# Four more split pairs, and four normalisations moved from VectorE to ScalarE, in a fused embedding, attention and mixture-of-experts kernel

## The reference, cut to what matters

```python
h = concat(fine_table[ids], softmax(cluster_table.T[ids] + b) @ coarse_table)
a = layernorm(h)                                   # x1 in the kernel
xn = rms_norm(a)
x2 = a + mem_scale * decayed_linear_attention(xn)
xn2 = rms_norm(x2)
h = h + x2 + op_scale * gelu(xn2 @ read_mix + bias) @ write_w
x3 = layernorm(h)
gates = normalised top-6 of softmax(x3 @ router_w.T + router_b)   # 64 experts, each with a capacity
out = h + sum over experts and 2 shared ones of gate * down(silu(x3 @ w_gate) * (x3 @ w_up))
```

## Time and profile before

| | |
|---|---|
| median of 3 runs | 718.52 us (718.14 to 718.71) |
| span of the profiled execution, first to last instruction | 716.0 us |
| what lies around the span, median less span | 2.5 us |
| busy: PE, PEld, DVE, ACT, POOL | 692.8, 524.7, 523.4, 350.6, 466.5 us |
| mean granted TensorE clock | 0.995 of full speed |

### The profile page before, as it was taken

How to read it: one execution, slowest core, us unless ns; L and a number is a source line. 1 busy time by engine, 2 the same in 40 slices (tenths; PEclk the granted TensorE clock), 3 DMA queues, 4 the chain that set the end, 5 groups by cost and what they waited for, 6 DMA issues and landing times.

```text
span 716.0 us, 9975 instructions
## 1 busy us (share of the span) xinstructions
PE 692.8 (97%) x3133; PEld 524.7 (73%) x3133; DVE 523.4 (73%) x1074; ACT 350.6 (49%) x609; POOL 466.5 (65%) x345
## 2 busy tenths in 40 slices
PE   7788899999999999999999999999999999999998
PEld 7666677777777777777777777777777777777775
DVE  5677686987768867887769877788678766674444
ACT  3543455446454374445553474544745435534432
POOL 5035477776677767685676776676775656676664
PEclk9999999999999999999999999999999999999999
DMA  5504232243323333333333433333333433334431
GB/s 204 226 1 128 71 118 104 85 133 105 111 106 114 114 108 99 120 113 102 118 103 101 128 103 103 118 110 109 114 105 102 125 103 105 115 112 124 138 123 60
DMA packets 48869, 80.17 MB, mean 112 GB/s; under 512 B 9520, under 2 KB 13744, under 8 KB 48816
## 3 DMA queue, kind: packets, MB, share of 16 engines
q1 hardware_dynamic: 47792, 77.44, 33.4%
q0 software_dynamic: 1024, 2.10, 1.2%
HBM read 76.35 MB, written 3.15 MB: 111 GB/s over the span
## 4 chain that ended last, share of the span: by engine, by line
PE 88%; DVE 4%; issue 3%; POOL 2%; ACT 1%; DVEq 0%; POOLq 0%
PE bank_y L467 16%; PE bank_g L481 8%; PE bank_g L482 8%; PE bank_g L483 8%; PE bank_u L483 8%; PE bank_u L481 8%; PE bank_u L482 8%; PE bank_y L464 4%; PE bank_y L462 4%; PE bank_y L461 4%; POOL hid L1040 1%; PE bank_f L408 1%; PE bank_f L386 1%; PE bank_f L402 1%; PE bank_f L445 1%
## 5 line engine op out<-in xcount | busy, mean ns | idle before, releaser
L1040 POOL TENSOR_TENSOR hid<-hid,gate_rows 128x512 f32<-128x512 f32 x256 | 374.2, 1470 | 195.4 <-DVE hid L881 193.0
L623 ACT ACTIVATE hid<-bank_g 128x512 f32<-128x512 f32 x264 | 156.6, 599 | 264.4 <-PE bank_g L483 261.8
L881 DVE TENSOR_TENSOR hid<-hid,bank_u 128x512 f32<-128x512 f32 x264 | 178.7, 681 | 128.3 <-PE bank_u L483 78.2
L481 PE MATMUL bank_g<-x_hi,gate_hi 128*128 128x512 f32 x264 | 142.9, 541 | 0.0
L467 PE MATMUL bank_y<-hid,w_down 128*128 128x512 f32 x272 | 138.7, 591 | 0.0
L887 DVE TENSOR_TENSOR hid_lo<-hid,hid_hi 128x512 fp32r<-128x512 f32 x128 | 110.2, 861 | 2.4 <-ACT hid_hi L629 2.4
L482 PE MATMUL bank_g<-x_hi,gate_lo 128*128 128x512 f32 x264 | 104.5, 396 | 0.0
L483 PE MATMUL bank_g<-x_lo,gate_hi 128*128 128x512 f32 x264 | 104.5, 396 | 0.0
L481 PE MATMUL bank_u<-x_hi,up_hi 128*128 128x512 f32 x264 | 103.9, 393 | 0.1
L483 PE MATMUL bank_u<-x_lo,up_hi 128*128 128x512 f32 x264 | 103.8, 393 | 0.0
L482 PE MATMUL bank_u<-x_hi,up_lo 128*128 128x512 f32 x264 | 103.8, 393 | 0.0
(11 more groups left out here) (209 smaller groups left out, 857.1 us busy)
## 6 DMA issues: line engine op xcount, KB each, us to landing
gate_rows<-gates_dram SPq DMA_DIRECT2D x512, 128.0 KB, 2.9
w_down<-down_t_dram SPq DMA_DIRECT2D x3, 704.0 KB, 14.5
out_dram<-later SPq DMA_DIRECT2D x7, 256.0 KB, 3.1
hid<-gate_t_dram SPq DMA_DIRECT2D x2, 704.0 KB, 5.8
gates_dram<-gates_t SPq DMA_DIRECT2D x8, 128.0 KB, 2.2
gate_rows<-up_t_dram SPq DMA_DIRECT2D x1, 704.0 KB, 5.7
later<-up_t_dram SPq DMA_DIRECT2D x1, 704.0 KB, 9.9
raw<-gate_t_dram SPq DMA_DIRECT2D x1, 704.0 KB, 11.0
```

The lines of the kernel that those rows point to most:

```text
L481: pe.matmul(o, w_hi[name][:, p, :], x3_hi[par][:, :], start=True, stop=False)
L623: act.activation(hid[:, slot(par, p), :], bank_g[(p + par) % 2][:, :], ACT.Silu).then_inc(sem("silu"), 1)
L881: dve.tensor_tensor(hid[:, s, :], hid[:, s, :], bank_u[(p + par) % 2][:, :], ALU.mult)\
L1040: pool.tensor_tensor(hid[:, s, :], hid[:, s, :], gate_rows[:, row, :], ALU.mult)\
```

## The change

Pairs 8, 12, 18 and 20 become split pairs too, so 20 of 33 are; the slots of `hid_hi` and `hid_lo` go by the running number of the split pair, still with two slots. `down_hi` and `down_lo` are made in nine pieces instead of one. For all sequences but the first, `x1`, `xn2` and `x3`, and from the third sequence on `xn`, are made by ScalarE activations (scale and bias are columns), at iterations 3, 11, 19 and 0. An activation adds its bias after it scales, so VectorE also makes the negated means, and GpSimd multiplies them by `inv1` or `inv3` into `shift1` and `shift3`. One run of filler in the prologue (`WARM_PREP`) grows from 9 transposes to 22.

```diff
-SPLITS = PAIRS // 2
+SPLIT_PAIRS = tuple(sorted(tuple(range(1, PAIRS, 2)) + (8, 12, 18, 20)))
+SPLITS = len(SPLIT_PAIRS)
...
-ACT_AT = dict(xn_hi=2, y_hi=4, z=6, ...
+ACT_AT = dict(xn=0, x1=3, xn2=11, x3=19, xn_hi=2, y_hi=4, z=6, ...
...
-WARM_START, WARM_PREP, WARM_EXP, WARM_COARSE, WARM_GATES = 20, (2, 9), 4, 26, 20
+WARM_START, WARM_PREP, WARM_EXP, WARM_COARSE, WARM_GATES = 20, (2, 22), 4, 26, 20
...
+        def split_runs():            # yields (slots, pairs) of each evenly spaced run: nine of them
+            at = 0
+            for _, group in itertools.groupby(enumerate(SPLIT_PAIRS), lambda jp: jp[1] - 2 * jp[0]):
+                pairs = [p for _, p in group]
+                yield slice(at, at + len(pairs)), slice(pairs[0], pairs[-1] + 1, 2)
+                at += len(pairs)
         def is_split(p):
-            return p % 2 == 1
+            return p in SPLIT_PAIRS
+        def split_slot(b, p):
+            return (SPLITS * b + SPLIT_PAIRS.index(p)) % SPLIT_RING
+        def split_slot_freed(b, p):
+            n = SPLITS * b + SPLIT_PAIRS.index(p) - SPLIT_RING
+            return PAIRS * (n // SPLITS) + SPLIT_PAIRS[n % SPLITS] + 1 if n >= 0 else 0
...                                   # act_late
+            if p == ACT_AT["xn"] and b > 1:
+                act.wait_ge(sem("shift1"), b)
+                for t in range(TILES):
+                    last = act.activation(xn[:, t, :], emb[par][:, t, :], ACT.Identity,
+                                          bias=shift1[:, 1, t:t + 1], scale=inv1[:, 1, t:t + 1])
+                last.then_inc(sem("xn"), 1)
+            if p == ACT_AT["x1"] and b:
...                                   # waits for shift1 and the x2 before; x1 with inv1[:, 0], in the same way
+            if p == ACT_AT["xn2"] and b:
+                act.wait_ge(sem("inv2"), b + 1)
+                for t in range(TILES):
+                    last = act.activation(xn2[:, t, :], x2[:, t, :], ACT.Copy, scale=inv2[:, t:t + 1])
+                last.then_inc(sem("xn2"), 1)
+            if p == ACT_AT["x3"] and b:
+                act.wait_ge(sem("shift3"), b)
...                                   # x3 with shift3 and inv3, in the same way
...                                   # act_hi
-            wait(act, "down_done", q - 2 * SPLIT_RING + 1)
+            wait(act, "down_done", split_slot_freed(b, p))
...                                   # ACT, prologue
-                    act.activation(down_hi[:, :, :], odd_pairs(w_down), ACT.Copy).then_inc(sem("down_hi"), 1)
+                    for j, pairs in split_runs():
+                        last = act.activation(down_hi[:, j, :], w_down[:, pairs, :], ACT.Copy)
+                    last.then_inc(sem("down_hi"), 1)
...                                   # dve_late
-            if p == DVE_AT["xn"]:
+            if p == DVE_AT["xn"] and b <= 1:
-            if p == DVE_AT["x1"]:
+            if p == DVE_AT["x1"] and b == 0:
-            if p == DVE_AT["xn2"]:
+            if p == DVE_AT["xn2"] and b == 0:
+                if b:                 # behind var3, iteration 17; the same for negated1 behind var1, iteration 18
+                    dve.tensor_scalar(negated3[:, :], mv3[:, :, 0], -1.0, None, ALU.mult).then_inc(sem("negated3"), 1)
-            if p == DVE_AT["x3"]:
+            if p == DVE_AT["x3"] and b == 0:
...                                   # pool_late, behind inv3; the same for shift1 behind inv1
+                if b:
+                    pool.wait_ge(sem("inv3"), b + 1)
+                    pool.wait_ge(sem("negated3"), b)
+                    pool.tensor_tensor(shift3[:, :], negated3[:, :], inv3[:, :], ALU.mult).then_inc(sem("shift3"), 1)
```

More of the change, by code:

```diff
@@ L18 @@
+import itertools
 from contextlib import ExitStack
@@ L59 @@
              router=23, gates_t=30)
-ACT_AT = dict(xn_hi=2, y_hi=4, z=6, ffn_t=5, squares=9, squares2=10, cluster_exp=10, exp_t=12, xn2_t=13, vals=14,
+ACT_AT = dict(xn=0, x1=3, xn2=11, x3=19, xn_hi=2, y_hi=4, z=6, ffn_t=5, squares=9, squares2=10, cluster_exp=10, exp_t=12, xn2_t=13, vals=14,
               x3_hi=21, router_exp=24)
@@ L162, in build @@
         inv1 = sb("inv1", [P, 2, TILES])
+        negated1 = sb("negated1", [P, TILES])
+        shift1 = sb("shift1", [P, 2, TILES])
         x1 = sb("x1", [P, TILES, D])
@@ L185, in build @@
         inv3 = sb("inv3", [P, TILES])
+        negated3 = sb("negated3", [P, TILES])
+        shift3 = sb("shift3", [P, TILES])
         x3, x3_t = xn, xn2_t
@@ L232, in slot @@
             return (p + PAIRS * par) % RING
[L234 to L235 removed]
+        def split_runs():
[4 more added lines that the diff above has]
+                at += len(pairs)
         def is_split(p):
[L239 removed]
+            return p in SPLIT_PAIRS
         def split_count(b, p):
[L243 removed]
+            return SPLITS * b + SPLIT_PAIRS.index(p) + 1
+        def split_slot(b, p):
[3 more added lines that the diff above has]
+            return PAIRS * (n // SPLITS) + SPLIT_PAIRS[n % SPLITS] + 1 if n >= 0 else 0
         def over(col, n):
@@ L281, in split_lo @@
                 dve.wait_ge(sem("down_hi"), 1)
-                dve.tensor_tensor(down_lo[:, :, :], odd_pairs(w_down), down_hi[:, :, :].bitcast(F32), ALU.subtract)\
-                   .then_inc(sem("down_lo"), 1)
+                for j, p in split_runs():
+                    last = dve.tensor_tensor(down_lo[:, j, :], w_down[:, p, :], down_hi[:, j, :].bitcast(F32),
+                                             ALU.subtract)
+                last.then_inc(sem("down_lo"), 1)
         def gate_row_loads(sp, b, r):
@@ L458, in down @@
                     pe.wait_ge(sem("down_lo"), 1)
-                k, j = (p // 2) % SPLIT_RING, p // 2
+                k, j = split_slot(b, p), SPLIT_PAIRS.index(p)
                 pe.wait_ge(sem("hid_hi"), split_count(b, p))
@@ L577, in act_late @@
             f0, f1 = bank_f
+            if p == ACT_AT["xn"] and b > 1:
[5 more added lines that the diff above has]
+            if p == ACT_AT["x1"] and b:
+                act.wait_ge(sem("shift1"), b)
+                act.wait_ge(sem("x2"), b)
+                for t in range(TILES):
+                    last = act.activation(x1[:, t, :], emb[par][:, t, :], ACT.Identity,
+                                          bias=shift1[:, 0, t:t + 1], scale=inv1[:, 0, t:t + 1])
+                last.then_inc(sem("x1"), 1)
+            if p == ACT_AT["xn2"] and b:
+                act.wait_ge(sem("inv2"), b + 1)
+                for t in range(TILES):
+                    last = act.activation(xn2[:, t, :], x2[:, t, :], ACT.Copy, scale=inv2[:, t:t + 1])
+                last.then_inc(sem("xn2"), 1)
+            if p == ACT_AT["x3"] and b:
+                act.wait_ge(sem("shift3"), b)
+                for t in range(TILES):
+                    last = act.activation(x3[:, t, :], h2[par][:, t, :], ACT.Identity,
+                                          bias=shift3[:, t:t + 1], scale=inv3[:, t:t + 1])
+                last.then_inc(sem("x3"), 1)
             if p == ACT_AT["xn_hi"]:
@@ L627, in act_hi @@
             act.wait_ge(sem("gated"), q + 1)
-            wait(act, "down_done", q - 2 * SPLIT_RING + 1)
-            act.activation(hid_hi[:, (p // 2) % SPLIT_RING, :], hid[:, slot(par, p), :], ACT.Copy)\
+            wait(act, "down_done", split_slot_freed(b, p))
+            act.activation(hid_hi[:, split_slot(b, p), :], hid[:, slot(par, p), :], ACT.Copy)\
                .then_inc(sem("hid_hi"), 1)
@@ L874, in dve_early @@
                    .then_inc(sem("var1"), 1)
+                if b:
+                    wait(dve, "shift1", b - 1)
+                    dve.tensor_scalar(negated1[:, :], mv1[:, :, 0], -1.0, None, ALU.mult).then_inc(sem("negated1"), 1)
         def dve_up(dve, b, par, p):
@@ L884, in dve_lo @@
         def dve_lo(dve, b, par, p):
-            k = (p // 2) % SPLIT_RING
+            k = split_slot(b, p)
             dve.wait_ge(sem("hid_hi"), split_count(b, p))
@@ L1015, in pool_late @@
                 pool.wait_ge(sem("var3"), b + 1)
+                wait(pool, "x3", b)
                 pool.tensor_tensor(inv3[:, :], var3[:, :], neg_half[:, 0:TILES], ALU.pow).then_inc(sem("inv3"), 1)
+                if b:
+                    pool.wait_ge(sem("inv3"), b + 1)
+                    pool.wait_ge(sem("negated3"), b)
+                    pool.tensor_tensor(shift3[:, :], negated3[:, :], inv3[:, :], ALU.mult).then_inc(sem("shift3"), 1)
         def pool_early(pool, b, p):
@@ L1020, in pool_early @@
                 pool.wait_ge(sem("var1"), b + 1)
+                wait(pool, "x1", b)
                 pool.tensor_tensor(inv1[:, :, :], var1[:, :, :], neg_half[:, :].rearrange("p (k t) -> p k t", k=2),
                                    ALU.pow).then_inc(sem("inv1"), 1)
+                if b:
+                    pool.wait_ge(sem("inv1"), b + 1)
+                    pool.wait_ge(sem("negated1"), b)
```

(2 more changed lines are left out.)

3 lines of the change are left out of this document (removed).

## The result

The changed kernel takes 722.97 us (median of 5 runs) against 718.52: 1.0072 of the time before, with an interval of 1.0052 to 1.0091. That is slower by 4.5 us where 9.8 us of gain were forecast.

What follows compares the result with a forecast made beforehand. TensorE's work plus its holes was taken to bound the kernel from the second sequence on; -5.1 - 2.45 - 1.9 - 1.6 + 1.1 + 0.1 = -9.85 us on the 716.0 span gave 706.15, with 2.5 around it 708.7 us; range 705.7 to 712.3.

Steps and rivals of the forecast that it cites:

- four splits: Down products of four more pairs, eight sequences: splitting saves TensorE 0.16 us each, -5.1 us (4.8 to 5.4).
- hole at the state, sequences 1 to 5: TensorE's idle time ahead of the state matmuls goes once ScalarE makes x1: -2.45 us (-1.9 to -2.45).
- sequence 0, hole and clock: The 2.24 us hole at the state shrinks by 1.9, and the clock staying full gives -1.6 us.
- prologue: down_hi in nine pieces lengthens the serial chain by 1.1 us (0.45 to 2.0); negated1 adds 0.1.
- ring of two, x3 on ScalarE: Copies waiting for a slot at pairs 9, 13, 19, 20, 21, and x3 at iteration 19: both costed at nothing.
- The step that failed: Costing at nothing: hid_lo with 2.4 us of slack; silu 19 ending about 444.7, TensorE's gate of pair 21 due 445.35.
- The ring as a rival: Other queued work makes down wait at forty tight pairs; 728.7 us at 0.5 us late each; chance 0.05 (over 720).
- x3 comes late: Slow shift3 or non-overlapping activations hold gate 21 up 0.5 us in each of seven sequences: 712.2 us; chance 0.08.
- Function tables: Rival: Identity needs table loads of 1283 ns, delaying silu 19 behind x3: +4.7 us, 713.4; chance 0.03.
- the slow stretch: Sequence 0's reduced TensorE clock, 74 to 78 us: full clock gives -1.6 us; rival that it stays, chance 0.13.

Runs made afterwards that it cites:

- f1: The changed kernel with ScalarE's router exponential at iteration 25 instead of 24, behind silu 24: 713.89 us, 0.9959 of the kernel before.
- g4: The changed kernel with three slots in hid_hi and hid_lo, pair 31 not split, and inv1 and shift1 at iteration 26 instead of 20: 714.02 us, 0.9952 of before.
- d1: The changed kernel with three slots in hid_hi and hid_lo instead of two, and pair 31 not split: 720.69 us, 1.0042 of the kernel before.
- e1: The changed kernel with GpSimd making inv1 and shift1 at iteration 26 instead of 20: 721.59 us, 1.0066 of the kernel before.
- e3: The changed kernel without pairs 18 and 20 split (only 8 and 12 added), all moves kept: 715.98 us, 0.9985 of the kernel before.
- e4: The changed kernel with x3 back on VectorE, the rest as changed: 720.80 us, 1.0052 of the kernel before.
- g3: The changed kernel with exponential at 25, split down weights in three pieces, gate transposes at 31 and VectorE's scan at 32: 719.47 us, 1.0030 of before.

## Why the prediction was wrong

Its terms on the span, in us; measured ones are from the iterations of the changed kernel over all eight sequences:

```
term                                   predicted  measured
four splits                               -5.1      -4.9   (0.16 + 0.14 + 0.16 + 0.15) x 8
hole at the state, sequences 1 to 5       -2.45     -3.5   0.70 x 5
sequence 0, hole and clock                -3.5      -1.4   92.33 - 92.55, less -0.6 of splits and 1.8 of iteration 25; but see below
prologue                                  +1.2      +1.3   start of the loop 48.51 to 49.80
ring of two, x3 on ScalarE                 0       +11.9   6 x 1.79 + 1.16 (sequence 6)
the rest, not in the prediction                     +2.0   what is left of the difference
sum                                       -9.85     +5.4   span 716.0 to 721.4
```

**The step that failed** is the costing of the ring and of `x3` at nothing. It checked whether each new or moved step came in time for TensorE: `hid_lo` 2.4 us early, the gate of pair 21 not held up. That was right; but for 0.4 us in one place no `down` waits, and no gate 21. But it asked only about the direct customers. The prediction named what is queued behind the waiting copy as "the next silu" and VectorE's "next product", and behind `x3` the copy of 17 and the product of 19, "both needed over a microsecond later". The product of 19 isn't needed by TensorE alone: GpSimd takes it, and behind it in GpSimd's queue stand `inv1` and the product of 20, then ScalarE's copies of 20 and 21, then VectorE's `hid_lo` of both and its router step, ScalarE's exponential, a table load and silu 24. The lateness was handed on from one to the next, and TensorE lost what exceeded the 0.41 us of margin. The rows ended at the gate of 21; from the start of `x3` to the gate that waited it is 461.01 - 445.40 = 15.6 us. The lateness of the product of 20 adds up, counted from the third gate matmul of pair 18 (438.88 and 441.41 us): the product of 19 starts 0.78 us later (6.14 to 6.92), `inv1` takes 0.44 more, and `shift1` with its gaps 0.37; together 1.6. At the router's addition it is 1.8, and TensorE then stands still for 1.50.

**The ring as a rival** had the right sign and the wrong place. It priced forty tight pairs with a wait ahead of `down`. What came was one wait per sequence ahead of a gate product, and nearly all of it needs three things: the splits of 18 and 20, GpSimd's late product or the missing slot, and an exponential ahead of silu 24. Take away the last (f1), or both of the middle (g4), and 1.77 or 1.69 of the 1.79 us go; either of the middle alone isn't enough (d1, e1), and without the splits 0.47 is left (e3).

**x3 comes late** was a rival for gate 21, which never waited. `shift3` took 0.20 us against 0.3 assumed, and the four activations 1.65 against 1.6. By e4 it is 0.44 us of the wait, elsewhere than thought.

**Function tables.** Loads stand on the lines of silu, the two exponentials and the gelu, as often as before, and none on those of the new Identity activations. Of the groups of lines of ScalarE in the changed kernel (busy us, mean ns of one) these are silu's loads and `x1`:

```profile
L669 ACT ACT_TABLE_LOAD x21 | 26.9, 1283 | 0.4
L610 ACT ACTIVATE x<-emb,shift,inv 128x128 f32<-128x128 f32 x28 | 11.5, 482 | 0.0
```

Silu still has 21 loads. This bears out what the prediction cited for it from the Trainium skill, "ScalarE: Activation LUTs", section "Table sets: the hidden batching unit", which no run had shown until now. What it cited from the section "Rules for kernel authors" of that page of the Trainium skill, that additions and multiplications belong on VectorE, is not borne out for these float32 tiles (the section's figure is for bf16): four took 2.07 and 3.22 us on VectorE and 1.65 on ScalarE.

**Sequence 0.** From 74 to 78 us the granted clock is 1.00 where it was 0.57, from 60 to 64 us 0.85 where it was 0.59. That looks like the forecast, but it can't be credited to the change. The kernel before with nothing but the exponential moved (f2) has the full clock behind a hole of 2.39 us. First the changed kernel, then f2:

```profile
74.00:78.00 4.00, 2.52 (x15) 2.18 (x15) 2.88 (x8) 0.82 (x2) 1.65 (x1) 1.00 0.30 92
74.00:78.00 4.00, 3.23 (x19) 2.86 (x20) 2.88 (x8) 1.12 (x2) 1.68 (x2) 1.00 0.11 39
74.77 0.91 PE L378 MATMUL bank_f<-z,shared 128*128 128x128 f32 x6 [2.39 <-issue]
```

From 60 to 64 us f2 has 1.00 too; the kernel before with the longer filler (g2) has 0.69 and 0.65, the repaired kernel (f1) 0.50 and 1.00. So the slow stretch comes and goes without the change, and the prediction had taken one profile's for the kernel's. In f2 sequence 0 takes 91.11 us against 92.55: that is as much as the -1.4 of the table, and no gain of the change in sequence 0 beyond its splits is shown. That the clock at the state came out as forecast was luck.

The hole did not go. With `x1` out of the queue, VectorE's split of the up weights starts while GpSimd is at a product, and took 2.72 us instead of 1.61, and the scores end at 74.69 + 0.74 = 75.43, still 1.48 us after TensorE is through (2.22 with the moves alone). GpSimd, VectorE and TensorE in the changed kernel:

```profile
70.67 1.41 POOL L1104 TENSOR_TENSOR hid<-hid,gate_rows 128x512 f32<-128x512 f32 x1 [0.61 <-DVE hid L934]
70.84 2.72 DVE L297 TENSOR_TENSOR up_lo<-later,up_hi 128x1408 fp32r<-128x1408 f32 x1
74.69 0.74 DVE L773 TENSOR_TENSOR shared<-bank_f,decay_mask 128x256 f32<-128x256 f32 x2
75.53 0.91 PE L400 MATMUL bank_f<-z,shared 128*128 128x128 f32 x6 [1.48 <-issue]
```

**The state in the other sequences** gave more than the idle time: 0.70 of iteration against 0.49 of hole. The row shows the first matmuls behind a hole slower too: six took 0.91 us behind it and 0.83 without.

With the term at pair 26 repaired (f1) the span is 711.8, not 706.15. Of these 5.65 us sequence 0 has 2.25 (92.55 to 90.70, less 0.6 of splits, is 1.25 for 3.5), the rest of the table 2.0, and iteration 30 gives back 2.2 (0.37 in six sequences); the state gave 1.05 more than forecast, and small terms make up what remains.

## What to carry to other kernels

Before a step is called free, follow its lateness through every queue until it reaches the bound engine, past the first customer: in-order queues hand it on, and a wait can appear fifteen us and four engines later. Look up the smallest margin on that way first (here 0.41 us at the silu behind the router's exponential). When a change loses though all its parts are in the trace, a table of iteration lengths finds the one place, and moving the waiting work one iteration can repair it without undoing the change (1.0070 of before to 0.9959 here). It can also do harm, as the gates an iteration later did (1.0030).

## What the runs showed of the hardware

Instructions of VectorE and GpSimd that overlap are stretched or held up, and by how much depends on the operands and on which began first. `hid_lo`, which reads two SBUF tiles, took 0.68 us in the changed kernel at 448.17, where GpSimd's product began behind it and took 1.68 instead of 1.29; it took 1.20 at 449.37, where the product was running already. The first of these and a later one that is needed below:

```profile
448.17 0.68 DVE L940 TENSOR_TENSOR hid_lo<-hid,hid_hi 128x512 fp32r<-128x512 f32 x1
451.68 0.68 DVE L940 TENSOR_TENSOR hid_lo<-hid,hid_hi 128x512 fp32r<-128x512 f32 x1
```

`up_lo`, also with two, took 1.61 and 2.72, `inv1` 1.64 and 2.08. VectorE's product with `bank_u`, which reads PSUM, stayed at 0.67 to 0.69 beside the same GpSimd work. The Trainium skill, "SBUF — State Buffer", section "SBUF: two separate sides", says that a VectorE instruction with two SBUF inputs and a GpSimd instruction that reads SBUF exclude each other, and that the one that starts first has the port for the whole instruction. The rows agree in three places, and in a fourth they don't. At 449.37 `hid_lo` had 449.37 + 1.20 - 450.01 = 0.56 us left when GpSimd's product ended, the long `hid_lo` of g3 also 0.56, near the 0.68 that it takes undisturbed, and `up_lo` 70.84 + 2.72 - 72.08 = 1.48 of 1.61. The one that doesn't fit is at 451.68: it took 0.68 us although `inv1` ran until 449.97 + 2.08 = 452.05.

Eighty bytes per partition of tiles that nothing reads made a sequence slower by 0.18 us in the 26 iterations that the table leaves out (64.35 to 64.53); a part came back in iteration 6, where the wait ahead of the state shrank (3.63 to 3.48). I read it as an effect of other addresses on TensorE's operands, but which operand it is, and why, was not tried. In the changed kernel, which has the same tiles, these iterations take 64.61; eight times the difference of 0.26 is 2.1 us, the size of the 2.0 that are left over in the sum. That the tiles are the cause there too is argued, not shown.
